# Finishing a chunk's states behind the second group of the next chunk, and the last chunk's in two parts

## The reference

```python
h = relu(layernorm(x));  x = x + rgcn(h)                 # 16 relations
h = relu(layernorm(x));  x = x + sage(h)                 # three SAGE layers
h = relu(layernorm(x));  x = x + gcn(h)                  # copy and product sums, degree norms
h = relu(layernorm(x));  x = x + gatv2(h)                # two attention layers

def sage_conv(x, src, dst, Wl, Wr, b):
    agg = segment_sum(x[src], dst) / max(count, 1)
    return agg @ Wl + x @ Wr + b                         # relu after the first two

def gcn(feat, ...):
    feat_n = feat * rsqrt(out_degree)
    h_src = feat_n[src]
    copy_sum  = segment_sum(h_src, dst)
    inner_sum = segment_sum(h_src * feat_n[dst], dst)
    return (copy_sum @ w1 + inner_sum @ w2) * rsqrt(in_degree)
```

## Time and profile before

| | us |
|---|---|
| median of three runs | 6364.63 |
| lowest and highest of them | 6355.12, 6367.59 |
| the profiled execution, its own time | 6354.62 |
| its span, first to last instruction | 6352.9 |
| third layer, from its first gathers' window to the patch gather | 2797 to 3376 |
| fourth layer, the same | 3391 to 3972 |

### The profile page before, as it was taken

How to read it: one execution, slowest core, us unless ns; L and a number is a source line. 1 busy time by engine, 2 the same in 40 slices (tenths; PEclk the granted TensorE clock), 3 DMA queues, 4 the chain that set the end, 5 groups by cost and what they waited for, 6 DMA issues and landing times. The chain is left out here.

```text
span 6352.9 us, 77087 instructions
## 1 busy us (share of the span) xinstructions
PE 3817.5 (60%) x19708; PEld 2604.5 (41%) x19708; DVE 4159.4 (65%) x13369; ACT 2294.0 (36%) x6083; POOL 4278.3 (67%) x4026
## 2 busy tenths in 40 slices
PE   3777788888288878866763444566466557760000
PEld 1444455555155545544543444455355423330000
DVE  6999799999544444434443665666599767765443
ACT  0000477777311111113334555222233279980000
POOL 5777777777677767767775775777300188884777
PEclk9999899999555555555555555788666689985555
DMA  1111344333233333334542454233244445552221
GB/s 40 50 47 47 120 158 158 115 112 100 70 101 106 89 94 97 97 94 128 152 139 81 147 151 132 92 93 94 70 162 173 154 116 141 150 126 78 88 87 63
DMA packets 413613, 684.98 MB, mean 108 GB/s; under 512 B 283685, under 2 KB 290444, under 8 KB 407978
## 3 DMA queue, kind: packets, MB, share of 16 engines
q1 hardware_dynamic: 282410, 542.14, 24.0%
q0 software_dynamic: 130944, 140.05, 11.1%
HBM read 310.94 MB, written 373.78 MB: 108 GB/s over the span
## 5 line engine op out<-in xcount | busy, mean ns | idle before, releaser
L711 POOL DMA_INDIRECT G<-states,srcq x1568 | 1608.5, 1026 | 488.5 <-issue 476.5
L1807 PE MATMUL PS<-ident,HH 128*128 128x128 f32 x2357 | 543.2, 380 | 936.5 <-ACT AT L2076 279.9
L1346 DVE SCALAR_TENSOR_TENSOR R<-R,same,G 128x64 f32<-128x64 f32 x1568 | 447.7, 286 | 829.0 <-DMA G<-states,srcq 645.3
L1807 PEld LDWEIGHTS PS<-ident,HH 128*128 128x128 f32 x2357 | 383.2, 197 | 1044.9 <-issue 481.9
L2076 ACT COPY AT<-PS 128x512 f32<-128x512 f32 (+1 forms) x494 | 283.7, 580 | 1047.6 <-PE PS L1822 719.4
L1822 PEld LDWEIGHTS PS<-WD,AT 128*128 128x128 f32 x2358 | 498.1, 312 | 178.9 <-issue 178.5
L824 POOL DMA_INDIRECT out_nodes<-O,dstq x392 | 432.2, 1103 | 187.5 <-issue 123.3
L1822 PE MATMUL PS<-WD,AT 128*128 128x64 f32 x2358 | 552.6, 412 | 0.0
L711 POOL DMA_INDIRECT EE<-node_info,srcq x392 | 412.5, 1052 | 134.4 <-issue 134.4
L711 POOL DMA_INDIRECT G<-states,srci x392 | 417.3, 1064 | 119.4 <-issue 118.8
L711 POOL DMA_INDIRECT PG<-in_x,dsti x392 | 406.6, 1037 | 119.4 <-issue 118.5
(11 more groups left out here) (413 smaller groups left out, 10053.8 us busy)
## 6 DMA issues: line engine op xcount, KB each, us to landing
states<-O SPq DMA_DIRECT2D x70, 896.0 KB, 3.8
HH<-states SPq DMA_DIRECT2D x56, 896.0 KB
total<-R SPq DMA_DIRECT2D x56, 896.0 KB, 3.7
XB<-resid SPq DMA_DIRECT2D x42, 896.0 KB, 6.1
states<-HH SPq DMA_DIRECT2D x28, 896.0 KB, 5.0
G<-states,srcq POOLq DMA_INDIRECT x1568, 2.5
resid<-XB SPq DMA_DIRECT2D x28, 896.0 KB, 6.8
xl_of_src<-O SPq DMA_DIRECT2D x14, 1792.0 KB, 6.9
```

Source lines behind the costliest of these rows:

```text
L711: return pool.indirect_dma_start(to, None, table_, bass.IndirectOffsetOnAxis(ap=idx, axis=0), bounds_check=bound, oob_is_err=False).then_i ...
L1346: row = dve.scalar_tensor_tensor(out=R[:, b, j * D:(j + 1) * D], in0=row_before, scalar=same[:, bass.ds(i * C + j, 1)], in1=G[:, b, j * D: ...
L1807: last = pe.transpose(PS[:, 4 + k, q * P:(q + 1) * P], HH[:, b, (g * G4 + q) * D2:(g * G4 + q + 1) * D2], ident[:])
```

## The change

DVE calls `finish` of chunk i - 1 from inside `rows_of` of chunk i, behind the operands of its second group (g == 1). ACT's square root moves from g == 2 to g == 1, its rows from steps 4 to 7 to steps 2 to 5. The last chunk is finished in two parts, `LAST_PARTS`: the first 20 columns when the puts of five groups are through, then the other 8. ACT does both parts behind the last put (`normed_last`). The counts of `s_done` and of the normalizations grow by one a layer. Two hunks that only carry these counts on into the node stage are left out.

```diff
@@ -343,7 +343,7 @@
         for k, layer in enumerate(LAYERS):
             normed = k >= 2
             plan(layer, ld=TURNS * 16, res=normed * TURNS * 16, st=(1 + normed) * TURNS * 16, tot=TURNS * 16, gath=TURNS * 16 * G4,
-                 scan=CHUNKS, ready=GROUPS * CHUNKS + 1, group=GROUPS * CHUNKS + 1, done=(CHUNKS + 1) * normed, ln=normed, carry=1,
+                 scan=CHUNKS, ready=GROUPS * CHUNKS + 1, group=GROUPS * CHUNKS + 1, done=(CHUNKS + 2) * normed, ln=normed, carry=1,
                  patch=(2 + normed) * 16, patched=(1 + normed) * 16)
         plan("att1", ld=TURNS * 16, st=TURNS * 16, gath=TURNS * 16 * G4, ready=CHUNKS, group=GROUPS * CHUNKS, patch=16)
         plan("sum1", ld=TURNS * 16, st=TURNS * 16, scan=CHUNKS, ready=CHUNKS + 1, group=GROUPS * CHUNKS + 1, carry=1,
@@ -359,6 +359,7 @@
             BAR[name] = len(BAR)
 
         AHEAD = 2
+        LAST_PARTS = ((0, 5 * G4), (5 * G4, 2 * G4))
 
 
         XL = [t.rearrange("p b n -> p (b n)") for t in (G[:], XB[:])]
@@ -584,7 +585,7 @@
                 body(CHUNKS - 2, 0, TURNS - 2, more=False)
                 body(CHUNKS - 1, 1, TURNS - 1, more=False)
                 if normed:
-                    sp.wait_ge(s_done, before[layer, "done"] + CHUNKS)
+                    sp.wait_ge(s_done, before[layer, "done"] + CHUNKS + 1)
                     states_out(CHUNKS - 1, 1)
                 for b in range(2):
                     sp.wait_ge(s_tot[b], before[layer, "tot"] + 16 * (TURNS + 1))
@@ -844,7 +845,7 @@
                 gather(HH[:, 0, D:D2], states[k][0:2 * ROWS, :], at_tail, ROWS - 1, s_patch)
                 if normed:
                     gather(XB[:, 0, 0:D], by_row(resid[k - 2]), at_tail, ROWS - 1, s_patch)
-                    pool.wait_ge(s_done, before[layer, "done"] + CHUNKS + 1)
+                    pool.wait_ge(s_done, before[layer, "done"] + CHUNKS + 2)
                 else:
                     pool.wait_ge(s_out, before[layer, "group"] + AHEAD + GROUPS * CHUNKS + 1)
                 if k < 3:
@@ -1302,22 +1303,26 @@
                 step(ts(left, r, col(RSIN_FT), None, ALU.mult))
                 return dve.scalar_tensor_tensor(out=right, in0=right, scalar=col(RSDST_FT), in1=left, op0=ALU.mult, op1=ALU.mult)
 
-            def new_states(k, layer, i, b):
-
-                total_, spread_, dev, inv, shift, diff = RLN
-                at = RNORMS + (k - 2) * CHUNKS + i
-                step(tt(XB[:, b, :], XB[:, b, :], O[:, b, 0:CD], ALU.add))
-                for j in range(C):
+            def new_states(k, layer, part, i, b, first, n):
+
+                some, rows_ = slice(first, first + n), slice(first * D, (first + n) * D)
+                total_, spread_, dev, inv, shift, diff = (t[:, some] for t in RLN)
+                stats_ = RSTATS[:, some]
+                at = RNORMS + (k - 2) * (CHUNKS + 1) + part
+                dve.wait_ge(s_out, before[layer, "group"] + AHEAD + GROUPS * i + (first + n) // G4)
+                step(tt(XB[:, b, rows_], XB[:, b, rows_], O[:, b, rows_], ALU.add))
+                for j in range(first, first + n):
                     last = dve.bn_stats(RSTATS[:, j, :], XB[:, b, j * D:(j + 1) * D])
                 step(last)
                 dve.wait_ge(s_scales, at)
-                tt(total_, RSTATS[:, :, 1], RSTATS[:, :, 4], ALU.add)
-                tt(spread_, RSTATS[:, :, 2], RSTATS[:, :, 5], ALU.add)
-                step(tt(diff, RSTATS[:, :, 1], RSTATS[:, :, 4], ALU.subtract))
+                tt(total_, stats_[:, :, 1], stats_[:, :, 4], ALU.add)
+                tt(spread_, stats_[:, :, 2], stats_[:, :, 5], ALU.add)
+                step(tt(diff, stats_[:, :, 1], stats_[:, :, 4], ALU.subtract))
                 step(dve.scalar_tensor_tensor(out=diff, in0=diff, scalar=D / 4.0, in1=diff, op0=ALU.mult, op1=ALU.mult))
                 tt(spread_, spread_, diff, ALU.add).then_inc(s_vars, 1)
                 dve.wait_ge(s_devs, at + 1)
-                dve.wait_ge(s_done, before[layer, "done"] + i)
+                if n == C:
+                    dve.wait_ge(s_done, before[layer, "done"] + part)
                 step(dve.reciprocal(inv, dev))
                 dve.scalar_tensor_tensor(out=shift, in0=total_, scalar=-0.5, in1=inv, op0=ALU.mult, op1=ALU.mult).then_inc(s_scales, 1)
@@ -1332,7 +1337,7 @@
             for k, layer in enumerate(LAYERS):
                 normed = k >= 2
 
-                def rows_of(i, it, b):
+                def rows_of(i, it, b, between=None):
                     step.reset()
                     dve.wait_ge(s_tot[b], before[layer, "tot"] + 16 * (it + 1))
                     step(dve.memset(col(SCR), 0.0))
@@ -1357,11 +1362,12 @@
                                 dve.wait_ge(s_ld[b], before[layer, "ld"] + 16 * (it + 1))
                             step(dve.memset(col(SCR), 0.0))
                         operands(k, i, b, g).then_inc(s_ready, 1)
+                        if g == 1 and between:
+                            between()
 
                 def finish(i, it, b):
                     dve.wait_ge(s_res[b], before[layer, "res"] + 16 * (it + 1))
-                    dve.wait_ge(s_out, before[layer, "group"] + AHEAD + GROUPS * (i + 1))
-                    new_states(k, layer, i, b)
+                    new_states(k, layer, i, i, b, 0, C)
 
                 def source_hots(i):
                     for h in range(2):
@@ -1386,15 +1392,17 @@
                     rows_of(0, 0, 0)
 
                     def turn(i, it, b, last_it):
-                        rows_of(i, it, b)
-                        finish(i - 1, last_it, 1 - b)
+                        rows_of(i, it, b, lambda: finish(i - 1, last_it, 1 - b))
 
                     with dve.Fori(0, TURNS - 1) as it:
                         turn(2 * it + 1, it, 1, it)
                         turn(2 * it + 2, it + 1, 0, it)
                     turn(CHUNKS - 1, TURNS - 1, 1, TURNS - 1)
                     step.reset()
-                    finish(CHUNKS - 1, TURNS - 1, 1)
+                    dve.wait_ge(s_res[1], before[layer, "res"] + 16 * TURNS)
+                    dve.wait_ge(s_done, before[layer, "done"] + CHUNKS - 1)
+                    for part, (first, n) in enumerate(LAST_PARTS):
+                        new_states(k, layer, CHUNKS - 1 + part, CHUNKS - 1, 1, first, n)
                 else:
                     def turn(i, it, b):
                         step.reset()
@@ -2116,20 +2124,33 @@
                         if g == GROUPS - 1:
                             last.then_inc(s_rscaled, 1)
 
+                normed_at = RNORMS + (k - 2) * (CHUNKS + 1)
+
+                def deviations(count, first, n):
+                    act.wait_ge(s_vars, normed_at + count)
+                    act.activation(RLN[2][:, first:first + n], RLN[1][:, first:first + n], ACT.Sqrt, bias=epsc[:], scale=1.0 / D).then_inc(s_devs, 1)
+
+                def normal_rows(b, first, n):
+                    for j in range(first, first + n):
+                        last = act.activation(O[:, b, j * D:(j + 1) * D], XB[:, b, j * D:(j + 1) * D], ACT.Relu,
+                                              bias=RLN[4][:, j:j + 1], scale=RLN[3][:, j:j + 1])
+                    return last
+
                 def normed_before(i, b, g):
-                    at = RNORMS + (k - 2) * CHUNKS + i
-                    total_, spread_, dev, inv, shift, diff = RLN
-                    if g == 2:
-                        act.wait_ge(s_vars, at)
-                        act.activation(dev, spread_, ACT.Sqrt, bias=epsc[:], scale=1.0 / D).then_inc(s_devs, 1)
-                    if 4 <= g < 8:
-                        if g == 4:
-                            act.wait_ge(s_scales, at)
-                        for j in range((g - 4) * (C // 4), (g - 3) * (C // 4)):
-                            last = act.activation(O[:, b, j * D:(j + 1) * D], XB[:, b, j * D:(j + 1) * D], ACT.Relu,
-                                                  bias=shift[:, j:j + 1], scale=inv[:, j:j + 1])
-                        if g == 7:
+                    if g == 1:
+                        deviations(i, 0, C)
+                    if 2 <= g < 6:
+                        if g == 2:
+                            act.wait_ge(s_scales, normed_at + i)
+                        last = normal_rows(b, (g - 2) * (C // 4), C // 4)
+                        if g == 5:
                             last.then_inc(s_done, 1)
+
+                def normed_last():
+                    for part, (first, n) in enumerate(LAST_PARTS):
+                        deviations(CHUNKS + part, first, n)
+                        act.wait_ge(s_scales, normed_at + CHUNKS + part)
+                        normal_rows(1, first, n).then_inc(s_done, 1)
 
                 put = out_rows(ACT.Relu if k < 2 else ACT.Identity, free)
                 if k == 2:
@@ -2144,13 +2165,11 @@
                             if i:
                                 normed_before(i, (i - 1) % 2, g)
```

(12 more changed lines are left out.)

## The result

The changed kernel takes 6321.36 us (median of 4 runs, 6320.67 to 6323.6), against 6366.11 of the kernel before on the same chip (6355.12 to 6373.02). The ratio is 0.9932, 95% interval 0.9915 to 0.9949. Measured twice more beside other kernels, it came to 0.9934 and 0.9939. The forecast was 6336 us with a range of 6318 to 6355. The profiled execution took 6320.67 us, with a span of 6319.0.

What follows compares the result with a forecast made beforehand. GpSimd's gathers were taken to pace both layers, so only the two tails could give time back. 15.6 + 15.4 - 2.8 = 28.2 us off the median 6364.6 gave 6336 us, range 6318 to 6355.

Steps and rivals of the forecast that it cites:

- The bound: Third and fourth layer: GpSimd sets the pace, 37.85 and 37.95 us a chunk; only the two tails can give back.
- F: End of the finish inside a chunk, counted from the scan end of the chunk before: 22 us third layer, 25 fourth.
- rival A: The finish makes a ring longer than GpSimd's chunk, so the kernel gets slower, some 6378 us; chance 0.06.
- The last put: Last product's put after the last scan: 12.7 us instead of 22.5 in third layer, 8.1 instead of 20.6 in fourth.
- The parts: Last chunk finished in two parts: rows end 11.35 us behind last put in third layer, 14.1 in fourth, instead of 17.1.
- rival B: Group 1 lands late, finish ends 8 to 10 us later; only the split gains, 6 us, 6359; chance 0.10.
- The tails' sum: Third layer 24.0 us instead of 39.6, gain 15.6; fourth layer 22.2 instead of 37.6, gain 15.4.
- What is given back: Chunk 12's residual add, moved up among the gathers, hits a thirteenth time in each layer: 2 x 1.4 = 2.8 us lost.
- the 7 either way: The 24 other moved adds in both layers: worth -7 to +7 us by their phase, taken as nothing.
- The row: Profile row: a 2.02 us DVE add stretches one gather to 2.37 us, or 2.09 in the fourth layer.
- Its ring for the third layer: Third layer: from a chunk's last put over the next finish to the next last put, 36.2 us against 37.85.
- the one that it had, over store and load: Fourth layer ring: store, loaded halves, scalings, square root, group 2, ACT's rows; 36.1 us against 37.95.

## Why the prediction was right

**The bound.** Right: GpSimd paces the layers, the idle part is still the issue gap, and nearly all that the change gave came from the two tails. That only the tails can give anything back was too narrow: the add in four pieces took 9.8 and 9.1 us off the gathers themselves.

**F.** Third layer: chunk 12's finish ends 21.8 us after the start of that chunk's last operands (3291.48 to 3313.24); 22 was taken. The number is right partly by luck. The working lets group 1 land up to 5 us late; its operands were done after 10.4 us, and VectorE then waited 3.79 us for chunk 12's last put (the add at 3305.67 above), a wait that the working of F does not have, though rival A does. In the fourth layer F is 19.5 us, not 25: group 0 waits 2.69 us for the scaled operands, and group 1 was there.

**The last put.** 12.4 us after the last operands for 12.7, and 7.5 for 8.1. The first follows the working: from the end of F to the put it takes 27.9 us for 28.6. In the fourth layer two errors cancel, and 8.1 came near by luck: F ends 5.5 us earlier than taken, and from there to the put it takes 26.4 us for 21, because the groups then wait for gathers (2.85 us ahead of the last one). The 7.5 us are what the first chunk takes too, which has no finish in front of it.

**The parts.** Rows end 10.9 us behind the last put for 11.35, and 13.3 for 14.1. The experiments add what the prediction did not see: alone the parts are worth 1.6 and 1.2 us, on top of the early finish 6.3 and 3.7, since a wait for the rows of chunk 12 stands ahead of them. For the 5.7 + 3.0 us that rival B has for the split alone, the run with the parts alone gives 2.8.

**The tails' sum.** 35.0 us instead of 31.0. 3.5 of the 4.0 missing us lie in the fourth layer: 0.6 from the put, 0.8 from the rows, and 2.1 that were not in the working: the last operands stand 3.3 us behind the last gather, 5.4 before.

**What is given back.** The count was right: thirteen adds, thirteen long gathers. The size was not: 1.4 us a layer were taken, and the busy time changed by -3.6 and +3.1 us, inside the 7 either way that the other adds were given. The adds now start at other moments between two gathers, and a 2.02 us add lengthens its gather by 0.6 to 1.8 us in the two profiles, where the working had 1.09 to 1.37 and 0.3 either way. The row was the right guide against the rule cited from the Trainium skill (SBUF — State Buffer, Who interferes with whom): by its inference a tensor_tensor leaves descriptor generation alone; every trace with a whole add shows gathers held past its end, by 0.87 us in the two pairs above.

**Rival A.** Its ring for the third layer can be read off: behind chunks 3, 5, 8 and 10 the finish starts on the chunk's last put, and the next chunk's follows 36.0 to 36.1 us later, for 36.2. GpSimd's chunk is longer, 37.5 us, and it waits for nothing. The margin was real: with 2.5 us more in the finish the rings outgrew the gathers, and the tails rose by 24.9 and 15.7 us. In the fourth layer the ring that did so was one that the prediction had not priced; the one that it had, over store and load, outgrew the gathers with the finish behind group four.

**The numbers.** 6321.36 us lies in the range, 3 us above its lower end and 15 below the forecast. By profiles the change is worth 33.9 us, by the layers alone 37.2 (31.8 to 37.3 with the other two profiles of the changed kernel), for 28.2 forecast: 4.0 from the tails, 3.3 from the gathers (0.5 gained where 2.8 was to be lost), 1.7 from elsewhere in the layers. The medians lie 44.8, 36.3 and 38.7 us apart in the three sets of runs. A sum stage that ends at the half clock goes with 11.8 us more, so a median gap can differ from the layers' by several us; whether the kernel before falls into it more often, its one profile, of the shorter kind, can't tell, and this stays open.

## What to carry to other kernels

Where one engine paces a loop, look at what happens between its last instruction and the stage's end: work that lags a chunk behind belongs early into the next chunk, and the last chunk may be cut, but only once no wait for the chunk before stands ahead of the cut. A long two-input VectorE operation beside indirect gathers is best cut in pieces that fit between the starts of two gathers (1.30 us apart here), as finely as the ring through it still fits into the pacing engine's chunk: compute that ring before, since each piece adds to it. Two halves of a change need not add up: here the tails lost 25.0 us by the early finish alone, 2.8 by the parts alone, and 35.0 by both.

## What was not expected of the hardware

A gather that begins while a two-input operation of VectorE runs (`tensor_tensor`, or the add as `scalar_tensor_tensor`) ends 0.87 us after that operation's end; one that has begun before the operation is not held by it. In the changed kernel's profile each of the 26 whole adds meets one gather that begins at least 0.05 us after it, and all 26 end 0.87 us behind their add, within 0.01 us. The same holds for shorter operations: counting every `tensor_tensor` of the two layers, the 0.42 us ones of `operands` among them, 107 gathers begin with more than 0.13 us of one still to come, all 107 end 0.87 us behind it, and of the 677 others four take more than 1.05 us (1.24 or 1.25).

So the price of an add is what is left of it when the next gather begins, less 0.13 us. With a gather every 1.30 us a 2.02 us add always meets one, and 13 cost 12.6 and 17.1 us a layer; a 0.61 us add often ends in time, and 52 cost 3.4 and 9.1; the 14 pieces of 0.3 us cost 0.8 in each layer. What in the chip makes a gather wait, no run here tells apart.
